# A convolution computed in two passes by images, and the second expert layer routed and sent by three groups

## The reference

```python
x = x + conv0(ln_channels(x))              # layer 0: squeeze-excite, attention 3x3, 1x1, norm
x = tokens(x); x = x + moe0(ln_tokens(x))  # 8 experts, top 2 of 8, 16384 tokens of 128
x = x + conv1(ln_channels(x))              # layer 1: depthwise 7x7, 128 channels
def conv1(x): return lax.conv_general_dilated(x, weight, (1, 1), ((3, 3), (3, 3)),
                       feature_group_count=128) + bias[None, :, None, None]
x = tokens(x); x = x + moe1(ln_tokens(x))  # 8 experts, top 2, 2560 places per expert
```

## Time and profile before

| | us |
|---|---|
| median of 3 runs (2270.89 to 2274.28) | 2272.59 |
| time of the profiled execution | 2273.36 |
| its span, first to last instruction | 2271.6 |
| mean granted PE clock over the span | 0.861 |

### The profile page before, as it was taken

One profiled execution on the slowest core, in us unless ns is written; L12 is line 12 of the kernel. 1 busy time (PEld: TensorE's weight loads), 2 busy tenths in 40 slices (PEclk: granted clock), 3 DMA queues, 4 the chain that ended last, 5 costly groups with the idle time before them and its releaser, 6 DMA issues.

```text
span 2271.6 us, 34896 instructions
## 1 busy us (share of the span) xinstructions
PE 1646.8 (72%) x9963; PEld 1386.0 (61%) x9963; DVE 1095.9 (48%) x4024; ACT 697.3 (31%) x1433; POOL 1023.3 (45%) x1041
## 2 busy tenths in 40 slices
PE   4899996998559999999999908870000029999944
PEld 3777775776549999899988808870000016666632
DVE  3465557655555445677678872285000002222257
ACT  0323322232124444555555511030000014444412
POOL 2000004442357777767544470017777745554520
PEclk9999998999779999999999958985555559999965
DMA  3165544653866665998789445601110012232258
GB/s 114 49 113 77 103 90 98 140 104 74 131 149 179 182 181 166 232 240 233 201 211 234 149 107 113 125 21 51 55 51 25 4 25 77 80 88 77 79 190 272
DMA packets 325342, 277.62 MB, mean 122 GB/s; under 512 B 72514, under 2 KB 301655, under 8 KB 325051
## 3 DMA queue, kind: packets, MB, share of 16 engines
q1 hardware_dynamic: 259898, 207.65, 38.6%
q0 software_dynamic: 31488, 55.94, 7.6%
q10 hardware_dynamic: 33792, 12.06, 2.0%
HBM read 167.37 MB, written 109.43 MB: 122 GB/s over the span
## 4 chain that ended last, share of the span: by engine, by line
PE 54%; DMA 15%; DVE 13%; issue 7%; POOL 6%; ACT 3%; SPq 1%; DVEq 1%; POOLq 0%; ACTq 0%
PE zp L708 8%; DMA slots_cap<-arena 7%; PE tp L865 7%; PE zp L984 6%; POOL slots_cap L596 5%; PE tp L875 4%; PE gp L887 3%; PE zp L887 3%; PE tp L997 3%; DMA out<-arena 3%; PE tp L790 2%; PE zp L875 2%; PE gp L805 2%; DMA slots<-arena 2%; DVE arena L1674 2%
## 5 line engine op out<-in xcount | busy, mean ns | idle before, releaser
L596 POOL DMA_INDIRECT slots<-arena x256 | 252.9, 988 | 550.7 <-DVE arena L1459 376.8
L636 POOL DMA_INDIRECT results<-arena x304 | 301.1, 990 | 188.3 <-DVE arena L1519 110.3
L596 POOL DMA_INDIRECT slots_cap<-arena x256 | 251.6, 983 | 228.1 <-issue 184.8
L708 PE MATMUL zp<-arena 128*128 128x256 f32 x1024 | 242.9, 392 | 45.9 <-ACT arena L1038 45.6
L977 PE MATMUL gp<-arena 128*128 128x128 f32 x160 | 26.6, 289 | 306.7 <-DVE arena L1674 306.7
L708 PEld LDWEIGHTS zp<-arena 128*128 128x128 f32 x1024 | 197.6, 196 | 76.3 <-ACT arena L1038 47.9
L671 POOL DMA_INDIRECT results<-arena x160 | 158.9, 993 | 170.8 <-DVE arena L1689 132.1
L977 PEld LDWEIGHTS gp<-arena 128*128 128x128 f32 x160 | 17.4, 143 | 340.5 <-issue 303.2
L865 PE MATMUL tp<-arena 128*128 128x256 f32 x912 | 223.7, 382 | 0.5 <-issue 0.5
L1534 DVE SCALAR_TENSOR_TENSOR arena<-tp,arena 128x256 f32<-128x256 f32 x304 | 134.8, 481 | 131.5 <-PE tp L875 110.8
L865 PEld LDWEIGHTS tp<-arena 128*128 128x128 f32 x912 | 162.8, 192 | 16.9 <-issue 0.9
(11 more groups left out here) (257 smaller groups left out, 3268.9 us busy)
## 6 DMA issues: line engine op xcount, KB each, us to landing
arena<-in_L_ffn_W SPq DMA_DIRECT2D x304, 192.0 KB
arena<-results SPq DMA_DIRECT2D x56, 512.0 KB, 5.1
arena<-slots SPq DMA_DIRECT2D x152, 134.0 KB
arena<-taps SPq DMA_DIRECT2D x64, 224.0 KB, 4.6
slots_cap<-arena SPq DMA_DIRECT2D x20, 536.0 KB
arena<-slots_cap SPq DMA_DIRECT2D x40, 268.0 KB, 2.9
arena<-in_x SPq DMA_DIRECT2D x8, 1024.0 KB, 8.7
arena<-arena SPq DMA_DIRECT2D x128, 64.0 KB
```

What stands on the lines that cost most here:

```text
L596: g.indirect_dma_start(slots[m], bass.IndirectOffsetOnAxis(ap=slot[:, k, blk:blk + 1].bitcast(U32), axis=0), rows[:, blk, :], None, bounds ...
L636: g.indirect_dma_start(results, bass.IndirectOffsetOnAxis(ap=row_at[:, q:q + 1].bitcast(U32), axis=0), y_tiles[:, q, :], None, bounds_chec ...
L708: t.matmul(dst, wg[:, j, k, :], xs[c][:, :, k, 0:P], start=(k == 0), stop=False)
```

## The change

The convolution of layer 1 runs twice over all 128 channels: first for blocks 0 to 95 (`AB`, columns `xn_ab`), as soon as the last pair of layer 0 is out, and then for blocks 96 to 127 (`xn_c`), behind the routing of the first 96. So the matrices `toep` are loaded twice (32 fills in place of 16), and there are 64 steps of 12 matmuls in place of 32. The sums of the last 32 blocks (`tail_sum`) stand behind DVE's steps 7 and 15 of the first pass. The bias is added by DVE with the convolution's sum, in four instructions a step in place of two; POOL's additions go. Layer 1 is routed in three groups of 48, 48 and 32 blocks; 48 blocks of the first group and 12 of the second are sent in bursts that wait for their landing (`CALM`). The first fill of `toep[0]` and its memset move into layer 0's pairs.

```diff
+R_BLOCKS, R_FIRST = 2 * G_BLOCKS, 2 * G_FIRST
+AB = G_FIRST[2]
+AB_STEPS, C_STEPS, C_BANKS = C // 4, C // 4, 6
+CALM = (48, 12, 0)
...
-        xn = arena.take(2, P, NBLK // 2)
-        toep = [arena.take(CG, 12, IMG) for _ in range(2)]
+        xn_ab = arena.take(P, AB)
+        toep = [arena.take(CG, 12, IMG)]
+        arena.at = phase + NBLK * P
+        toep.append(arena.take(CG, 12, IMG))
         y_in8 = [arena.take(KB, 2, P) for _ in range(2)]
+        xn_c = arena.take(P, NBLK - AB)
...
 # SP, first chunk of layer 0's results
                         sp.dma_start(conv_b, conv_bias.rearrange("(a c) -> a c", a=1).partition_broadcast(P)
                                      ).then_inc(sem("convb_in"), 16)
+                        sp.wait_ge(sem("taps_out"), 16 * IMG)
+                        sp.wait_ge(sem("toep_zero"), 1)
+                        load_toep(0)
...
-            for n in range(TAIL):
-                if n >= 2:
-                    sp.wait_ge(sem("x2_ready"), CHUNKS + n - 1)
+            for n in range(2):
+                load_results(y_in8, f"y_in{n}", CHUNKS // 2 + n, n)
+            sp.wait_ge(sem("toep_zero"), 2)
+            for g in range(1, 6):
+                load_toep(g)
+            for n in range(2, TAIL):
+                sp.wait_ge(sem("x2_ready"), CHUNKS + n - 1)
                 load_results(y_in8, f"y_in{n % 2}", CHUNKS // 2 + n, n % 2)
-            sp.wait_ge(sem("taps_out"), 16 * IMG)
-            for g in range(2):
-                sp.wait_ge(sem("toep_zero"), g + 1)
+            for g in range(6, 2 * NCG):
                 load_toep(g)
-            for g in range(2, NCG):
-                load_toep(g)
...
 # POOL, before the first send of layer 0's third group (T = 48)
+                            g.memset(toep[0].rearrange("p a b c -> p (a b c)"), 0.0).then_inc(sem("toep_zero"), 1)
...
-            with pool.Fori(0, CHUNKS // 2) as n:
-                add_bias(n, 2 * n + 2)
-            with pool.Fori(CHUNKS // 2, NBLK // KB) as n:
-                add_bias(n, n + CHUNKS // 2 + 1)
+            g.memset(toep[1].rearrange("p a b c -> p (a b c)"), 0.0).then_inc(sem("toep_zero"), 1)
...
-            for r in (GROUPS, GROUPS + 1):
+            for r in range(GROUPS, 2 * GROUPS):
                 pool.wait_ge(sem("slots_ready"), r + 1)
-                for n in range(GB):
+                calm = CALM[r - GROUPS]
+                for n in range(0, calm, BURST):
+                    burst(r, n, BURST)
+                for n in range(calm, R_BLOCKS[r]):
                     for k in range(2):
                         send(r, n, k)
...
 # PE
-            pe.wait_ge(sem("xn3_ready"), CHUNKS + TAIL)
+            pe.wait_ge(sem("xn3_ready"), CHUNKS)
             pe.wait_ge(sem("y_ready"), NP)
+            def conv(step, src, images, bank):
+                s, n = (step // 2) % 2, images * KB
+                if step % 2 == 0:
+                    pe.wait_ge(sem(f"toep_in{s}"), 64 * (step // 4 + 1))
+                for c in range(4):
+                    w = toep[s].rearrange("p c a x -> p c (a x)")[:, 4 * (step % 2) + c]
+                    cols, dst = src[:, 4 * (step % AB_STEPS) + c, :], bank[:, n * c:n * c + n]
+                    t.matmul(dst, w[:, P:2 * P], cols, start=True, stop=True)
+                    dk = dst.rearrange("p (b k) -> p b k", k=KB)
+                    sk = cols.rearrange("p (b k) -> p b k", k=KB)
+                    t.matmul(dk[:, :, 0:KB - 1], w[:, 0:P], sk[:, :, 1:KB], start=False, stop=True, skip_group_check=True)
+                    m = t.matmul(dk[:, :, 1:KB], w[:, 2 * P:3 * P], sk[:, :, 0:KB - 1], start=False, stop=True,
+                                 skip_group_check=True)
+                m.then_inc(sem("conv_done"), 1)
+            for step in range(AB_STEPS):
+                if step >= 8:
+                    pe.wait_ge(sem("x3_ready"), step - 7)
+                conv(step, xn_ab, AB // KB, banks[step % 8])
...
+            for turn in range(last_ab + 1):
+                router(turn, turn == last_ab)
             ranks(GROUPS)
+            for m in range(C_STEPS):
+                if m == C_BANKS:
+                    ranks(GROUPS + 1)
+                if m >= C_BANKS:
+                    pe.wait_ge(sem("x3_ready"), AB_STEPS + m - C_BANKS + 1)
+                conv(AB_STEPS + m, xn_c, (NBLK - AB) // KB, banks[m % C_BANKS])
+            pe.wait_ge(sem("x3_ready"), AB_STEPS + C_STEPS)
+            chunk_up(AB // KB, 0)
+            for turn in range(last_ab + 1, NBLK // KB // 2):
                 router(turn, turn == NBLK // KB // 2 - 1)
-            ranks(GROUPS + 1)
+            ranks(GROUPS + 2)
...
 # DVE
+            def conv_add(step, first, last, bank):
+                dve.wait_ge(sem("conv_done"), step + 1)
+                chan = 4 * (step % AB_STEPS)
+                n = last - first
+                for c in range(4):
+                    at = xt[:, first:last, chan + c]
+                    done = v.scalar_tensor_tensor(out=at, in0=bank[:, n * c:n * c + n], scalar=conv_b[:, chan + c:chan + c + 1],
+                                                  in1=at, op0=ALU.add, op1=ALU.add)
+                done.then_inc(sem("x3_ready"), 1)
+            for step in range(AB_STEPS):
+                conv_add(step, 0, AB, banks[step % 8])
+                if step in (7, 15):
+                    tail_sum(step // 8)
...
             router(0)
+            route(GROUPS)
             router(1)
-            route(GROUPS)
+            route(GROUPS + 1)
+            dve.wait_ge(sem("xn3_ready"), CHUNKS + TAIL)
+            for m in range(C_STEPS):
+                conv_add(AB_STEPS + m, AB, NBLK, banks[m % C_BANKS])
             router(2)
-            router(3)
-            route(GROUPS + 1)
+            route(GROUPS + 2)
```

More of the change, by code:

```diff
@@ L125 @@
 TAIL = G_BLOCKS[2] // KB
-SENT = [2 * sum((G_BLOCKS + (GB, GB))[:n + 1]) for n in range(GROUPS + 2)]
+R_BLOCKS, R_FIRST = 2 * G_BLOCKS, 2 * G_FIRST
+SENT = [2 * sum(R_BLOCKS[:r + 1]) for r in range(2 * GROUPS)]
+AB = G_FIRST[2]
+AB_STEPS, C_STEPS, C_BANKS = C // 4, C // 4, 6
 F1 = 512
@@ L272, in metaformer @@
         arena.at = phase
-        lg_off4 = arena.take(TURN4, E8)
+        lg_off4 = arena.take(MOST, E8)
         tnc4 = [arena.take(KB, P) for _ in range(2)]
@@ L605, in burst @@
                         send(r, n, k)
-                last = SENT[r] - 2 * G_BLOCKS[r] + 2 * (first + blocks) - 1
+                last = SENT[r] - 2 * R_BLOCKS[r] + 2 * (first + blocks) - 1
                 for j in range(last - 2 * blocks + 1, last + 1):
@@ L1117, in weights @@
                 act.wait_ge(sem("gap"), r + 1)
-                first, blocks = (G_FIRST + (0, GB))[r], (G_BLOCKS + (GB, GB))[r]
+                first, blocks = R_FIRST[r], R_BLOCKS[r]
                 part = slice(first, first + blocks)
@@ L1150, in normalise @@
                 for blk in range(first, last):
-                    half, place = (1, blk) if blk < NBLK // 2 else (0, blk - NBLK // 2)
-                    done = A(xn[:, half, :, place], xt[:, blk, :], ACT.Identity,
+                    done = A(xn_ab[:, :, blk] if blk < AB else xn_c[:, :, blk - AB], xt[:, blk, :], ACT.Identity,
                              bias=mean_2[:, blk:blk + 1], scale=rstd_2[:, blk:blk + 1])
@@ L1197, in router @@
                 logits_out(2 * turn + 1, 1)
+            last_ab = AB // KB // 2 - 1
             chunk_out(0, 0)
-            repeat(act, 0, EARLY, router)
+            for turn in range(last_ab + 1):
+                router(turn, turn == last_ab)
             weights(GROUPS)
-            for turn in range(EARLY, NBLK // KB // 2):
+            weights(GROUPS + 1)
+            chunk_out(AB // KB, 0)
+            for turn in range(last_ab + 1, NBLK // KB // 2):
                 router(turn, turn == NBLK // KB // 2 - 1)
-            weights(GROUPS + 1)
+            weights(GROUPS + 2)
             per = CT // QT
@@ L1612, in _ @@
                 scales(o, mean, rstd, 2 * KB, True, True, 2)
-            dve.wait_ge(sem("biased"), NBLK // KB)
-            with dve.Fori(0, NCG // 4) as turn:
-                for n in range(8):
-                    dve.wait_ge(sem("conv_done"), 8 * turn + n + 1)
-                    for h in range(2):
-                        half = slice(NBLK // 2 * h, NBLK // 2 * (h + 1))
-                        other = slice(NBLK // 2 * (1 - h), NBLK // 2 * (2 - h))
-                        at = xt[:, half, bass.ds(32 * turn + 4 * n, 4)]
-                        last = v.tensor_tensor(at, at, banks[n].rearrange("p (c k) -> p k c", c=4)[:, other, :], ALU.add)
-                    last.then_inc(sem("x3_ready"), 1)
@@ L1628, in _ @@
-            dve.wait_ge(sem("x3_ready"), C // 4)
-            def router(turn):
-                o = Order(dve, sem("dve_router"), turn, 6 + STAT_LINKS + RSQRT_LINKS)
-                blks = slice(TURN4 * turn, TURN4 * turn + TURN4)
-                wide = lambda z: z.to_broadcast([P, TURN4, E8])
```

(18 more changed lines are left out.)

95 lines of the change are left out of this document (34 added, 61 removed).

## The result

The changed kernel takes 2343.73 us (median of 4 runs, 2341.57 to 2344.43), the kernel before 2271.74 (4 runs): a ratio of 1.0317 [1.0301, 1.0332]. I had predicted 2280, in a range of 2260 to 2302. "Slower" was right, the size was not: 70.7 us in the span (2342.3 against 2271.6) where my sum had 7.4.

A forecast was written before the change was run, and what follows sets the result against it. Layer 1's sends, one after the other behind a serial stretch, were taken to bound the kernel; +2.6 - 43.8 - 2.9 + 51.5 = +7.4 on 2273.36 gave 2280.8, against the median 2280; range 2260 to 2302.

The forecast's parts named there:

- Part 1: Layer 0's pairs: the memset of toep[0] ahead of POOL's send passes whole to PE's wait, +2.6 us (0 to +6).
- Part 2: Layer 1's first convolution pass ends near 1428.7, without part 1, against 1472.45: 43.8 us saved (61 to 32).
- Part 3: From the first pass's end to layer 1's first send: 47.2 us against 50.1, so -2.9 (ends 45 and 50).
- Part 4: Layer 1's sends: 20 waiting bursts cost 38.5 us, waits beside second-pass fills 13, sum +51.5 (38 to 128).
- Part 5: Second pass and third routing: hidden behind the sends, done by 1651 against 1777, cover 126 us, cost 0.
- The rival that the second pass comes late: Third group's sends would wait for its routing; needs 126 us more, 2300 at a guess of 20 beyond; chance 0.05.
- my other end: First pass: no stall at groups 1, 2 and 6, or PE faster, ending at 1411, 61 us saved.

The follow-up runs named there:

- wide pass: Changed kernel with the first pass's matmuls streaming 128, 112 and 112 columns in place of 96, 84 and 84: 2293.86 us, 1.0095 of the kernel before.
- fillers throughout: Changed kernel with unread 128x512 matmuls ahead of the first pass's waits for fills (set 4): 2392.20 us, 1.0011 of the kernel before.
- the bursts alone: Kernel before with the first 60 blocks of its first half sent in 20 waiting bursts of six sends (set 2): 2425.39 us, ratio 1.0145.
- the last run: Changed kernel with both passes wide, 12 bursts, toep[0] fill a chunk later, fills 1 and 2 ahead of results' loads: 2284.99 us, 1.0045 of the kernel before.
- the kernel with 96 columns of set 4: Kernel before with 96 of 128 columns computed and eight unread 128x512 matmuls ahead of the convolution: 2451.51 us, 1.0264 of the kernel before.

## Why the prediction was wrong

**Part 1 (+2.6; measured +5.9).** The memset passed to POOL's next send as 2.06 (867.77 against 865.71). The fill of `toep[0]`, which I let go out "during SP's wait", lengthened that wait: the last scatters, started at 907.67, were landed at SP's load at 913.79, 6.1 later, where before it was 3.1 (905.34 to 908.43). The fill moved away gave 3.5 of the wait back (9.30 to 5.83). I had named +6 as an end and taken the memset alone.

**Part 2 (-43.8; measured +10.7 beside part 1).** This is the step that failed, in its sentence "so I keep 5.36 for 96 columns and for 32". That holds at a clock of 1.00 (steps 0 and 1: 5.6 for a group), but I had carried the clock over from the kernel before as if it came with PE being busy: after group 1's idleness I allowed 2.8 us of half clock, and the stream never left it. At 0.50 a group takes 10.24, the fills' waits vanish, and 30 steps take 154. With that pace my own terms give 1327 + 2.6 + 154 + 1.2 = 1485 for the pass and 2334 for the kernel (an estimate), most of what was missing. Both halves are needed: with wider columns the pause cost little (wide pass), with PE's pauses filled the narrow columns cost nothing (fillers throughout). The wide pass ended at 1440.7, 9 behind my figure, of which 4.7 are its later start (1315.2 for 1310.5): the fills' pace and the stall behind the loads of results were about right, and group 1's start at 1334 as well (I had 1327, plus part 1's 6).

**Part 3 (-2.9; measured -1.9)** was right: 48.1 from the pass to the first send, predicted 47.2. The transposes and logits behind the pass brought the clock from 0.50 to 1.00 by 1494, some 5 us behind the pass.

**Part 4 (+51.5; measured +55.8)** was close in its sum, and in part by luck. The quiet price (38.5) held about: the bursts alone cost 31 in time and 41 in the sends. Of the waits beside fills I had ten at 3.6, 13 in all; they were twelve at 2.77 in the mean, 5.9 in all, and 9.5 came from three long ones that I hadn't priced, one of them beside fills. That bursts are dearer beside faster fills, the last run shows.

**Part 5 (0)** held, in part by luck. The second pass ran at 0.50 and ended at 1707.96, 92 to 116 later than I had it; its routing was done near 1740, 89 late. But the third group's sends begin at 1840 (the last 64), 63 later than my 1777, since the first pass was late as well. So 100 us of my 126 of cover were left. The rival that the second pass comes late did come true, but in kernels without bursts and on a slower chip. I had weighed it only with what bursts leave, and had not asked what the bursts are for.

**The chances.** I gave nothing to a slower PE in the first pass: my other end was a faster one. A range from the rows would have needed the question which work had brought the clock to 1.00 in the earlier trace rows, and whether the new stream is that work.

## What to carry to other kernels

When a change makes the moving side of the matmuls narrower, price them at either granted clock, and look in the profile for the clock of a stretch of that shape before counting on the higher one; that PE is busy is no sign of it. If the trace has no such stretch, the half clock is a rival of its own. Columns that nobody reads, or fillers in PE's waits, cost nothing where fills set the pace, and are a cheap trial. Waits in a queue of small transfers may guard something that the profile of one chip doesn't show: try their removal on more than one chip before believing the gain.

## What the runs showed of the hardware

- A 100% busy PE at a granted clock of 0.50 for 154 us (96 columns), and a fall from 1.00 to 0.50 with no pause (32 columns, 1525 to 1531). Streams of 128 and 112 columns fell behind waits too (1422 in the kernel before, 1390 in the wide one) and were at 1.00 again 3.4 us later.
- Records of 28 to 128 columns came 111 to 117 ns apart at 1.00 and 213 to 227 at 0.50 (medians by width; a step of 24 takes 2.68 and 5.12 us). Narrower ones bought nothing at either level. The Trainium skill's page "TensorE: Matmul & The Clock Gate" has two rules on this: "Back-to-back issue gap" has, for matmuls alone and not for pairs with a weight load, a warm spacing that falls with the columns streamed; "LDWEIGHTS (loading the stationary operand)" gives 128 weight columns 107 ns, in a formula without the streamed columns. The trace agrees with the second at 1.00: 112, against 42.5 ns by the first at 96 columns (an estimate from that page). Even from this kernel's own wide records at 1.00, 216 ns for 256 columns and 429 for 512, 96 columns would have some 83 (an estimate). At 0.50 it doesn't agree: 213, and the formula knows no second value.
- Chips differ. The kernel before took 2271 to 2273 in two sets and 2389 to 2394 in two others. Some 103 of those 120 us lie ahead of the convolution (PE's first work there at 1473.21, in the kernel with 96 columns of set 4, where the earlier trace rows have 1369.77). They aren't spread over it: the same PE records in the kernel with 20 bursts (set 2) are within 2 us of the kernel before until 670, and 104 to 106 behind from about 1120 on (times of the kernel before). That is the stretch in which POOL issues sends and scatters beside the pairs; its last send is at 1099 in the one and at 1204 in the other. On such a chip unpaced indirect sends went with PE's instructions coming 2.80 us apart. The cause of either was not tried.
